# A fused two-layer transformer on one core: one output bank, a shared ring of score banks and a token-major projection in the first attention, wide masks in the second

## What is computed

```
h = layernorm(x) * (1 + ca) + sa
# attention 0
q = h @ Wq + bq;  k = (h @ Wl + bl) @ Wk + bk;  v = (h @ Wl + bl) @ Wv + bv
attn = softmax(q k^T * DIM_HEAD ** -0.5)
x = x + ga * ((attn @ v) @ Wo + bo)          # ga: one gate per batch and feature
...feed-forward, then layer 1:
# attention 1
out = g * A_mem + (1 - g) * softmax(causal(q k^T)) @ v
x = x + ga * (out @ Wo.T + bo)
...mixture of experts
```

## Time and profile before

| what | value |
|---|---|
| median of 3 runs (lowest, highest) | 896.36 us (893.45, 896.53) |
| profiled execution | 895.1 us, span of its instructions 893.3 us |
| PE busy | 743.3 us (83%), 5927 matmuls |
| DVE busy | 613.4 us (69%) |
| ACT busy | 563.2 us (63%) |
| POOL busy | 359.6 us (40%) |
| DMA | 42.05 MB, mean 47 GB/s, nearly all on SP's queue |
| attention 0 | from about 21 us to 341 us of the span |
| attention 1 | from about 577 us to 723 us |

### The profile page before, as it was taken

How to read it: one execution, slowest core, us unless ns; L and a number is a source line. 1 busy time by engine, 2 the same in 40 slices (tenths; PEclk the granted TensorE clock), 3 DMA queues, 4 the chain that set the end, 5 groups by cost and what they waited for, 6 DMA issues and landing times. The chain is left out here.

```text
span 893.3 us, 17728 instructions
## 1 busy us (share of the span) xinstructions
PE 743.3 (83%) x5927; PEld 538.4 (60%) x5927; DVE 613.4 (69%) x1483; ACT 563.2 (63%) x1258; POOL 359.6 (40%) x449
## 2 busy tenths in 40 slices
PE   3376888888888874789999997589999967999996
PEld 3222444444444334789889997367777755888784
DVE  3075777777777835677877763367767856888884
ACT  0214777777777753668878886277677734565553
POOL 3542534534421001051121000477877643777674
PEclk9999999999999985899999999599999987999998
DMA  5355354443442001300000000000000060464430
GB/s 138 47 73 73 64 67 66 66 68 52 55 54 41 2 3 14 119 1 2 1 1 1 1 1 1 2 2 1 2 1 3 18 176 4 112 187 114 118 107 23
DMA packets 76927, 42.05 MB, mean 47 GB/s; under 512 B 9026, under 2 KB 74916, under 8 KB 76580
## 3 DMA queue, kind: packets, MB, share of 16 engines
q1 hardware_dynamic: 76836, 40.89, 22.9%
HBM read 25.66 MB, written 2.24 MB: 31 GB/s over the span
## 5 line engine op out<-in xcount | busy, mean ns | idle before, releaser
L579 DVE TENSOR_REDUCE att_negmax<-att_p_max 128x2 f32<-128x512 f32 x256 | 164.6, 685 | 74.2 <-PE att_p_max L459 73.2
L663 ACT ACTIVATE att_probs<-att_p_sT 128x1024 f32<-128x1024 f32 x128 | 129.3, 1022 | 47.1 <-PE att_p_sT L465 46.1
L2047 POOL TENSOR_TENSOR moe_z_lo<-moe_z,moe_z_hi 128x512 fp32r<-128x512 f32 x64 | 96.6, 1524 | 54.8 <-ACT moe_z_hi L2000 53.0
L459 PE MATMUL att_p_max<-att0p_QK 48*128 48x256 bf16 x512 | 91.6, 288 | 26.9 <-DVE att_negmax L579 11.4
L939 POOL TENSOR_TENSOR ffn0s_rstd<-ffn0s_var_eps,top_minus_half 128x2 f32<-128x2 f32 x16 | 11.2, 698 | 197.3 <-DVE ffn0s_var_eps L926 197.3
L465 PE MATMUL att_p_sT<-att0p_QK 51*128 51x256 bf16 x512 | 86.0, 281 | 0.2 <-DMA att0p_QK<-att_maxT 0.2
L893 PE MATMUL ffn0s_p_h<-ffn0s_u_hi,top_ffn_all 128*128 128x256 f32 x256 | 70.9, 309 | 16.5 <-DVE ffn0s_u_lo L1154 16.2
L459 PEld LDWEIGHTS att_p_max<-att0p_QK 48*128 48x128 bf16 x512 | 33.2, 96 | 77.3 <-DVE att_negmax L579 46.8
L488 PE MATMUL att_p_o<-att_probs,att0p_V 128*32 128x256 f32 x1024 | 70.5, 394 | 10.0 <-ACT att_probs L663 9.0
L1154 DVE TENSOR_TENSOR ffn0s_g_lo<-ffn0s_g,ffn0s_g_hi 128x512 fp32r<-128x512 f32 x64 | 49.0, 781 | 42.0 <-ACT ffn0s_g_hi L1098 40.7
L2038 DVE TENSOR_TENSOR moe_z<-moe_act_u,top_ffn_all 128x512 f32<-128x512 f32 x64 | 73.5, 1149 | 2.2
(11 more groups left out here) (248 smaller groups left out, 2037.5 us busy)
## 6 DMA issues: line engine op xcount, KB each, us to landing
top_ffn_all<-combine SPq DMA_DIRECT2D x32, 512.0 KB, 6.9
att0p_QK<-att_parts SPq DMA_DIRECT2D x192, 64.0 KB
top_X<-in_L_attn_x SPq DMA_DIRECT2D x4, 512.0 KB, 6.9
att_raw<-in_L_ffn_h_w SPq DMA_DIRECT2D x8, 256.0 KB, 2.8
out_x<-top_X SPq DMA_DIRECT2D x8, 256.0 KB, 2.3
top_wo_all<-gates SPq DMA_DIRECT2D x1, 1024.0 KB, 5.2
ffn0s_raw_gu<-in_L_ffn_w SPq DMA_DIRECT2D x1, 1024.0 KB, 8.0
prep_wmod<-in_L_wmod SPq DMA_DIRECT2D x2, 384.0 KB, 3.7
```

The source lines that it names most:

```text
L459: mm = pe.matmul(p_max[u % 2][:, i, :], QK[r][rows, g, 0, i * P:(i + 1) * P], QK[r][rows, g, 1, :], start=True, stop=True)
L579: dve.tensor_reduce(negmax[:, :, w, g], p_max[u % 2][:], AX.X, ALU.max, negate=True).then_inc(maxed, 1)
L663: act.activation(probs[g % 2][:, t % 2], p_sT[t % 2][:], ACT.Exp).then_inc(exped, 1)
L2047: pool.tensor_tensor(z_lo[e % RING][:], z[e % RING][:], z_hi[e % RING][:].bitcast(F32), ALU.subtract).then_inc(z_lo_ready, 1)
```

## The change

In attention 0:

- The bank `p_o` becomes `[P, 2, S]` and takes all heads of a batch. V is laid out so that two groups of heads add into the same 32 columns (zeros where the other's are). `pe_pv` is cut in halves of 8 instructions, one after each of the slots 14, 15, 2, 3, 6, 7, 10, 11. ACT copies once for a batch, PE turns it in 4 pieces in place of 8, DVE divides with one reciprocal and one product.
- A "ring": the two banks of `p_max` are used in one order, `RING`, by the tiles of the maxima and by two more users for each batch, the turned outputs (`"O"`) and the projection (`"out"`). The counters `filled` and `drained` replace `scored`, `maxed` and others.
- The projection is token-major: `OTn` times `k.wo1_all[:, b, :]`, that is Wo with the gate of the batch multiplied in (`pool_gate_wo`), straight into a bank from which DVE adds to `x`. `act_y` and `pe_turn_y` go. The gated bias is added to `x` by POOL (`pool_bias`). The gates are turned once, stored to DRAM and loaded back as rows on all partitions, 4 batches at a time.
- The chain that splits the maxima (`neg_chain`, 4 instructions) moves from DVE to POOL, ahead of all else in POOL's step.
- The slots are dealt anew (below); the scores of `s` begin in slot 8, not 6. The end of a batch moves to step `n - 5`, so there is one more step.
- SP's order in step `n` becomes: `sp_max(n - 3)`, `sp_stack(n - 1)`, in steps 1 to 4 two loads of gates, from step 5 on a group of weights. All steps are written out, there are no loops.

In attention 1 the mask is added with one product for each head that covers both halves; the bias goes out of PE's `pe_out` and is added to `x` by POOL after its normalisation, and DVE's add waits for that. `prepare` sets V to zero with whole memsets. Feed-forward 0 no longer stores the gates of layer 1 to DRAM.

```diff
-PES = {"ln": 0, "max_turn": 2, "qk": 3, "O0": 5, "v": 8, "O1": 9, "back": 11, "out": 12, "turn_y": 14,
-       "pv_s": (11, 15), "pv_t": (3, 7)}
-DVE = {"negmax": 0, "stats": 2, "O0": 6, "O1": 10, "add": 15}
-ACTS = {"hT": 0, "maxT": 1, "qk": 3, "v": 7, "OTn": 11, "y": 12, "OT_s": (11, 15), "OT_t": (3, 6)}
+PES = {"back": 1, "max_turn": 3, "out": 5, "ln": 6, "q": 9, "k": 10, "v": 13, "O": 14,
+       "pv_s": {14: (0, 0), 15: (0, 1)}, "pv_t": {2: (1, 0), 3: (1, 1), 6: (2, 0), 7: (2, 1), 10: (3, 0), 11: (3, 1)}}
+SCORES = 8
+DVE = {"negmax": 0, "out": 5, "stats": 8, "O": 14}
+ACTS = {"OTn": 1, "maxT": 1, "hT": 6, "qk": 10, "OT": 10, "v": 12, "parts": 13}
+GATES = 4
...
         def pe_max_turn(pe, b):
             pe.wait_ge(neg_ready, b + 1)
-            if not isinstance(b, int) or b + 3 < B:
-                wait_apart(pe, k, hT_ready, b + 4)
-            else:
-                at_least(pe, x_added, b - 1)
+            at_least(pe, OTn_ready, b - 1)
+            pe.wait_ge(v_ready, min(b + 3, B))
...
+        def dve_normalise_O(dve, b):
+
+            at = RING["O", b]
+            groups = bank(at)[:].rearrange("p i (m c) -> p (i m) c", c=32)
+            dve.wait_ge(filled, at + 1)
+            at_least(dve, drained, RING["O", b - 1] + 1 if b else 0)
+            dve.reciprocal(recip[:], groups[:, :, 2 * DH0:2 * DH0 + 2]).then_inc(recip_ready, 1)
+            dve.wait_ge(recip_ready, b + 1)
+            at_least(dve, OTn_turned, b)
...
-        def sp_step(sp, n, r):
+        def sp_step(sp, n):
             if batch_valid(n - 3):
-                sp_max(sp, n - 3, (r - 3) % NB)
-            if 0 <= n - 1 < WEIGHT_GROUPS:
-                at_least(sp, w_loaded, weights_loaded(n - 1))
-                at_least(sp, w_lo_ready, n - len(raw))
-                for to, of in weight_loads[n - 1]:
+                sp_max(sp, n - 3, (n - 3) % NB)
+            if batch_valid(n - 1):
+                sp_stack(sp, n - 1, (n - 1) % NB)
+            if n == 1:
+                sp.wait_ge(gate_rows_ready, 1)
+                sp.dma_start(k.gates_dram, gate_rows[:]).then_inc(gates_stored, 16)
+                sp.wait_ge(gates_stored, 16)
...
+            g = n - FIRST_GROUP
+            if 0 <= g < WEIGHT_GROUPS:
+                at_least(sp, w_loaded, weights_loaded(g))
+                at_least(sp, w_lo_ready, g + 1 - len(raw))
+                for to, of in weight_loads[g]:
                     sp.dma_start(to, of, allow_slow_non_contiguous=True).then_inc(w_loaded, 16)
-            if batch_valid(n):
-                sp_stack(sp, n, r)
...
         def pool_step(pool, n, r):
+            if batch_valid(n - 3):
+                neg_chain(pool, n - 3)
+            if batch_valid(n - 3):
+                pool_bias(pool, n - 3)
+            if 0 <= n - 2 < B // GATES:
+                pool_gate_wo(pool, n - 2)
+            if 0 <= n - FIRST_GROUP - 1 < WEIGHT_GROUPS:
+                pool_split_weights(pool, n - FIRST_GROUP - 1)
             if batch_valid(n + 1):
                 pool_normalise(pool, n + 1)
-            pool_parts(pool, n, r)
-            if 0 <= n - 2 < WEIGHT_GROUPS:
-                pool_split_weights(pool, n - 2)
+            if batch_valid(n):
+                pool_parts(pool, n, r)
...
             for i in range(NT):
                 out = p_n[:, i * D:(i + 1) * D]
-                pe.matmul(out, OT[b % 2][:, i * P:(i + 1) * P], k.wo1_all[:, b, :], start=True, stop=False)
-                mm = pe.matmul(out, k.ones_row[0:1, :], k.gbo1_row[0:1, b, :], start=False, stop=True)
+                mm = pe.matmul(out, OT[b % 2][:, i * P:(i + 1) * P], k.wo1_all[:, b, :], start=True, stop=True)
             mm.then_inc(y_made, 1)
```

More of the change, by code:

```diff
@@ L416, in weights_loaded, with bank @@
             return 16 * sum(len(g) for g in weight_loads[:groups])
+        RING = {}
+        for n in range(LAST):
+            for slot in range(TILES):
+                if slot == PES["out"] and batch_valid(n - 5):
+                    RING["out", n - 5] = len(RING)
+                if slot == PES["O"] and batch_valid(n - 4):
+                    RING["O", n - 4] = len(RING)
+                if batch_valid(n - 2):
+                    RING["max", n - 2, slot] = len(RING)
+        def bank(at):
+            return p_max[at % 2]
         def head_rows(w, n):
@@ L479, in pe_max_turn @@
             mm.then_inc(max_turned, 1)
[L481 to L488, removed]
-                                   probs[g % 2][:, h // 2, h % 2, j, :], start=(j == 0), stop=(j == NT - 1))
-            mm.then_inc(pv_made, 1)
@@ L517, in pe_step @@
         def pe_step(pe, n, r):
-            f, m, s, t = n, n - 2, n - 3, n - 4
+            f, m, s, t, y = n, n - 2, n - 3, n - 4, n - 5
             rm, rs, rt = (r - 2) % NB, (r - 3) % NB, r
             for slot in range(TILES):
+                if slot == PES["back"] and batch_valid(y):
+                    pe_turn_back(pe, y)
+                if slot == PES["max_turn"] and batch_valid(s):
+                    pe_max_turn(pe, s)
+                if slot == PES["out"] and batch_valid(y):
+                    pe_out(pe, y)
@@ L547, in pe_step @@
[L547 to L558 removed]
+                    pe_pv(pe, t, rt, *PES["pv_t"][slot])
@@ new lines, in dve_add, with dve_step @@
+        def dve_add(dve, b):
+            at = RING["out", b]
+            dve.wait_ge(filled, at + 1)
+            dve.wait_ge(bias_added, b + 1)
+            x = k.X[:, b * NT:(b + 1) * NT, :]
+            dve.tensor_tensor(x, x, bank(at)[:, 0, :].rearrange("p (i d) -> p i d", i=NT), ALU.add).then_inc(drained, 1)
+        def dve_step(dve, n):
+            f, m, s, t, y = n, n - 2, n - 3, n - 4, n - 5
+            for slot in range(TILES):
+                if slot == DVE["out"] and batch_valid(y):
+                    dve_add(dve, y)
+                if slot == DVE["O"] and batch_valid(t):
+                    dve_normalise_O(dve, t)
@@ L627, in dve_step @@
                     dve_stats(dve, f + 1)
-                if slot == DVE["add"] and batch_valid(t):
-                    dve_add(dve, t)
         def act_hT(act, b):
@@ L833, in _ @@
             pool_normalise(pool, 0)
-            for n in range(WHOLE.start):
-                pool_step(pool, n, n % NB)
-            for turn in range(0, LOOPS):
-                for r in range(NB):
-                    pool_step(pool, turn * NB + (WHOLE.start + r), r)
-            for n in range(WHOLE.stop, B):
+            for n in range(B + 3):
                 pool_step(pool, n, n % NB)
@@ L843, in _ @@
         def _(pe):
-            for n in range(WHOLE.start):
-                pe_step(pe, n, n % NB)
-            for turn in range(0, LOOPS):
-                for r in range(NB):
-                    pe_step(pe, turn * NB + (WHOLE.start + r), r)
-            for n in range(WHOLE.stop, LAST):
+            pe_turn_gates(pe)
+            for n in range(LAST):
                 pe_step(pe, n, n % NB)
@@ L853, in _ @@
         def _(act):
-            for n in range(WHOLE.start):
-                act_step(act, n, n % NB)
-            for turn in range(0, LOOPS):
-                for r in range(NB):
-                    act_step(act, turn * NB + (WHOLE.start + r), r)
-            for n in range(WHOLE.stop, LAST):
+            act_gate_rows(act)
+            for n in range(LAST):
                 act_step(act, n, n % NB)
@@ L864, in _ @@
             dve_stats(dve, 0)
[L865 to L871 removed]
+            for n in range(LAST):
+                dve_step(dve, n)
                 if n == B:
```

336 lines of the change are left out of this document (161 added, 175 removed).

## The result

The changed kernel takes 937.27 us (median of 4, 932.71 to 940.65), the kernel before beside it 896.41: ratio 1.046, interval 1.041 to 1.051. So it is slower by twice what I forecast (916 us); the range of 888 to 942 holds it. The profiled execution took 938.08 us, with a span of 936.3 us where the one before had 893.3, and a mean granted clock of 0.875 where that had 0.950.

The account below looks back on a forecast made before the run. It took attention 0 to become bound by waiting for the q and k stack: +36.3 there, -0.5 last tiles, -6.5 tail, -9.0 attention 1, or +20.3 on 895.1, giving 915.4, stated as 916 us; range 888 to 942.

Parts of the forecast that it names:

- Filling, up to step 4: Attention 0's first steps: later stack start, gate loads and freed maxima DMAs leave step 4 starting at 83 us, as before.
- The stack's loop, 19.3 us: Attention 0: slot 0, maxima, their DMAs, twelve stack DMAs, next slot 0 set the pitch: 19.3 us with weights, 17.9 without.
- Its lead: Attention 0, from slot 0 of a step to the issue of the maxima: 3.4 us, bounds 2.9 and 4.1.
- my 14.2: Attention 0: time for a stack's twelve DMAs to land when a group of weights shares the queues, 14.2 us; 12.8 without.
- POOL's chain isn't late: Attention 0: POOL's four small instructions end 0.8 to 3 us after the last reduction, within a several-us wait before slot 0.
- the rival: Attention 0: POOL's chain, behind the previous step's parts, delays `max_turn` 1 to 2 us a step; 930 to 940 us, chance 0.04.
- The clock rival: Attention 0: waiting 4 to 5 us in slot 0 lowers PE's clock every step; pitch near 21.5, 944 us, chance 0.09.
- the case to which I gave 0.72: Attention 0's pitch is set by the wait for the q and k stack; whole 890 to 946 us, chance 0.72.
- DVE's saving, a hand-over at 14.8 us: Attention 0: DVE's own work falls from 14.4 to 12.9 us a step; the DVE-PE hand-over alone would run at about 14.8.
- the stack keeps up: Attention 0: twelve DMAs land in under 9.7 us, so the pitch is the hand-over's 14.8; 857 us, chance 0.15.
- The tail: End of attention 0: POOL passes the sums by and the last sums stand behind one division, saving 6.5 us, between 4 and 9.
- Attention 1: Fewer row and mask products, part given back by DVE: 0.6 us in each of 15 steps, 9 us saved, between 0 and 14.

Follow-up runs that it names:

- the kernel with the filler: Against the changed kernel, 13 unread PE products of 128 columns were added per step, ahead of the first two tiles; 937.87 us, ratio 1.046.
- the kernel with both repairs: Changed kernel with the chain on DVE, weights issued ahead of a stack in its own step, and the maxima's DMAs issued by ACT; 918.96 us, ratio 1.025.
- the kernel with the stack in its own step: Changed kernel with the chain on DVE, batch n's stack issued in step n ahead of the weights, and the maxima's DMAs issued by ACT; 923.36 us, ratio 1.034.

## Why the prediction was wrong

- **Filling, up to step 4: right.** I had the first slot of step 4 at 83 us; it starts at 81.5, and the maxima go out at 85.36, as before (85.21).
- **The stack's loop, 19.3 us: right as a size, wrong as the bound.** It measures 19.45 and 19.81 with the chain out of the way. Its lead, 3.4 us with a bound of 4.1, is 4.4 to 5.6 in the changed kernel (slot 0 at 232.49, maxima at 238.04), beyond the bound, since chain and clock are in it. The stack took 13.9 us for my 14.2, so that two small errors cancel in the 19.45.
- **The step that failed: "POOL's chain isn't late", and in the rival "those parts end before PE's wait does".** I placed the parts of the step before against a wait of several us in slot 0 that I had derived myself. Had I timed the parts from their own releaser, the first part in slot 13, they would have ended 2.3 us after the chain was due, as above. DVE waited 2.87 us for the chain in each of the 11 steps. The wait of several us that was to hide it was 1.5 to 2.1 us where it came at all, because at the low clock the steps were so long that the stack had landed. In the kernel with the filler, at full clock, those parts did end before PE's wait, so the statement fails together with the clock. The rival had the right place, but a price of 1 to 2 us and a chance of 0.04.
- **The clock rival: right in what it saw, wrong as a separate case.** It gave a pitch of 21.5 and 944 us at 0.09; 22.05 and 937 came. That its figures came so near is in part luck, for its cause was not the stack's wait alone. The late chain idles PE by 2.76 us, the clock falls, the step grows longer, the stack's wait that would have covered the chain is gone, and DVE waits for the chain again. Two rivals that work together were priced as if only one could hold, and both lay outside the case to which I gave 0.72. 2.75 us in each of 11 steps are 30 us, more than the whole miss of 21.
- **DVE's saving, a hand-over at 14.8 us: open.** With DVE relieved of the chain the kernel before stays at 16.68, so there I had subtracted DVE's work from a pitch that DVE does not set. But with the chain on DVE and eight DMAs three steps in a row took 15.6 to 15.7 us (154.52 to 201.41), which is below 16.67 and near my 14.8 with the 0.84 us of the chain put back. The kernel with the stack out of the loop runs at 16.8 at full clock, with ACT's two issues in each step. None of these shows 14.8 itself, on which the rival "the stack keeps up" at 857 us was built. It cost the forecast nothing, as the stack's loop hid it. What sets 16.67 before is left open.
- **The tail: right.** The answer to the earlier trace rows, changed kernel:

```profile
388.63 0.34 SPq L858 DMA_DIRECT2D flag<-att_lo_any  x1
395.66 0.26 SPq L860 DMA_DIRECT2D att_lo_row<-flag  x1
```

  From the last reduction, done at 374.5, to the next block at 400.5 it is 26.0 us, before 32.0 (310.3 to 342.3): -6.0, and I had -6.5.
- **Attention 1: right sign, too small.** -16.4 us where I took -9 and allowed 14. The answer to the earlier trace rows is

```profile
693.20 0.67 PE L1482 MATMUL att_p_t<-att_hT,top_wq 128*128 128x256 f32 x2
...
701.12 0.67 PE L1482 MATMUL att_p_t<-att_hT,top_wq 128*128 128x256 f32 x2
```

  7.92 us, not 8.8. By the starts of PE's groups in one step, the projection with its bias took 677.13 to 678.69 before and takes 698.25 to 698.70: 1.11 us less, where I had counted 2 x 0.41 for the two row pairs. The pairs of real weights ran slower too when they alternated with those of one row (0.39 and 0.49 us, against 0.61 for four in a row). Scores with masks took 675.04 to 676.69 and take 696.50 to 697.81: 0.34 less, and I had 0.15. And DVE gave nothing back: PE's wait in a step is 0.39 us, before 0.35.

## What to carry to other kernels

When work moves to another engine, time what stands ahead of it on that engine from its own releaser, in the new order of slots, and not from the wait which you expect elsewhere. Where each of two waits can idle PE, put them and the clock into one loop and sum once round it, at both levels of the clock; as separate rivals they look small. A wait that covers another one covers it only as long as it is there. And split a change by its parts on the chip: here attention 1 alone was 17 us faster and attention 0 hid it.

## What the runs showed of the hardware

- An idle stretch of PE of 2.76 us, and in the kernel with both repairs one of 2.21, stood ahead of a fall of its granted clock from 1.00 to 0.50 that lasted some 10 us. Behind two shorter ones, of 1.81 and 0.63 us with two tiles' products and a turn between them, it lasted 17 us. The Trainium skill describes such a loop (TensorE: Matmul & The Clock Gate, HAM oscillation) with DMAs as what is awaited; here the traces show the same fall where PE waited for DVE.
- The same chain costs DVE more while POOL works beside it. Groups by shape, 120 to 260 us, first the kernel before, then the chain on DVE in the changed kernel:

```profile
L589 DVE CAST att_negparts<-att_negrest 128x32 bf16<-128x32 f32 x8 | 1.4, 180 | 0.3
L585 DVE CAST att_negparts<-att_negmax 128x32 bf16<-128x32 f32 x8 | 1.4, 172 | 0.0
```

```profile
L607 DVE CAST att_negparts<-att_negrest 128x32 bf16<-128x32 f32 x8 | 3.8, 473 | 0.3
L603 DVE CAST att_negparts<-att_negmax 128x32 bf16<-128x32 f32 x8 | 3.5, 437 | 0.3
```

  The casts take 0.44 and 0.47 us instead of 0.17 and 0.18, where POOL's parts run at the same time. In the kernel with the stack in its own step, where POOL then stood waiting for weights, they took 0.19 and 0.22. The Trainium skill has a cause for it: VectorE and GpSimd share a pair of SBUF ports as an exclusive lock (SBUF — State Buffer, SBUF: two separate sides). The numbers fit that, but no run here tells it from another cause.
- Two DMAs issued by ACT held its next exponential back by 1.6 us in each step, while SP issued such a pair in 1.54. Twelve stack DMAs on SP's queue held the maxima that stood behind them back by up to 7.4 us as PE saw it; with the maxima issued by ACT no wait of the same kind was over 1.5 us from 100 to 290 us.
